# A fused attention and mixture-of-experts layer: sums of key blocks added in pairs on GpSimd, router input turned by DMA

## The reference

```python
x = x + tanh(g_xattn) * attention(layernorm(x), ctx)   # softmax(Q K^T / sqrt(32)) V, then Wo
x = x + tanh(g_ffn) * moe(layernorm(x))                # top-2 of 8 experts, capacity 1229 of 8192 places
# moe: probs = softmax(x @ Wr + br); gates, ids = top_k(probs, 2); each expert silu(x W1 + b1) W2 + b2
```

## Time and profile before

| | |
|---|---|
| median of 3 runs | 1811.75 us (1811.48 to 1812.64) |
| the profiled execution, its own time | 1810.6 us |
| its span (first to last instruction) | 1808.9 us |
| attention, start to last product of it on TensorE | 0 to 902.6 us |
| busy TensorE, VectorE, ScalarE, GpSimd | 96%, 60%, 44%, 24% of the span |
| matmul records | 10371 |

### The profile page before, as it was taken

One profiled execution on the slowest core, in us unless ns is written; L12 is line 12 of the kernel. 1 busy time (PEld: TensorE's weight loads), 2 busy tenths in 40 slices (PEclk: granted clock), 3 DMA queues, 4 the chain that ended last, 5 costly groups with the idle time before them and its releaser, 6 DMA issues.

```text
span 1808.9 us, 29536 instructions
## 1 busy us (share of the span) xinstructions
PE 1727.7 (96%) x10371; PEld 827.7 (46%) x10371; DVE 1076.8 (60%) x2087; ACT 798.2 (44%) x1093; POOL 434.4 (24%) x424
## 2 busy tenths in 40 slices
PE   6999999999999999999918999999999999999998
PEld 4324243342423334243305657475665647565563
DVE  6777867778776777867687625345252525434231
ACT  4553735547364554735423426153342516244240
POOL 2332434224343332431201211211021121112101
PEclk9999999999999999999958999999999999999999
DMA  6334263433425433243123542625263362626312
GB/s 227 106 86 125 71 167 113 102 119 100 144 93 142 137 93 116 81 114 109 42 100 105 133 124 100 168 87 154 71 174 80 120 148 88 179 50 177 75 44 29
DMA packets 214608, 203.19 MB, mean 112 GB/s; under 512 B 121813, under 2 KB 162913, under 8 KB 210457
## 3 DMA queue, kind: packets, MB, share of 16 engines
q1 hardware_dynamic: 193432, 181.80, 33.1%
q0 software_dynamic: 21120, 20.67, 6.6%
HBM read 134.57 MB, written 43.63 MB: 99 GB/s over the span
## 4 chain that ended last, share of the span: by engine, by line
PE 84%; DVE 10%; issue 3%; ACT 2%; POOL 1%; DMA 0%; SPq 0%; DVEq 0%; ACTq 0%; POOLq 0%
PE psum L1598 23%; PE psum L1574 21%; PE psum L1369 7%; PE psum L1376 6%; PE psum L1360 6%; PE psum L1350 6%; PE psum L1340 6%; PE psum L1462 5%; PE psum L1387 3%; DVE mx L938 2%; DVE reached L1092 1%; DVE x2hl L1012 1%; DVE x2hl L1014 1%; DVE stats L890 1%; DVE x2n L897 1%
## 5 line engine op out<-in xcount | busy, mean ns | idle before, releaser
L1598 PE MATMUL psum<-w,hT 128*128 128x512 f16 (+1 forms) x1920 | 415.7, 379 | 0.0
L1574 PE MATMUL psum<-xgT,w 128*128 128x308 f16 (+1 forms) x3072 | 408.1, 293 | 0.6 <-DVE xgT L1193 0.6
L938 DVE TENSOR_REDUCE mx<-psum 128x1 f32<-128x512 f32 x512 | 330.2, 683 | 104.1 <-PE psum L1350 102.5
L1574 PEld LDWEIGHTS psum<-xgT,w 128*128 128x128 f16 x3072 | 296.2, 97 | 109.3 <-DVE xgT L1193 1.1
L788 ACT ACTIVATE pt<-psum 128x1024 f32<-128x1024 f32 x256 | 255.0, 1022 | 116.4 <-PE psum L1360 116.4
L1598 PEld LDWEIGHTS psum<-w,hT 128*128 128x128 f16 (+1 forms) x1920 | 199.3, 104 | 213.8
L864 ACT ACTIVATE h<-psum,b1c 128x308 f32<-128x308 f32 (+1 forms) x256 | 117.9, 511 | 342.0 <-PE psum L1574 341.6
L1214 DVE TENSOR_TENSOR hT<-h,hT 128x615 f16<-128x615 f32 x128 | 102.5, 801 | 210.1 <-ACT hT L867 210.1
L681 POOL DMA_INDIRECT out_dram<-y,idx_now x40 | 87.6, 2191 | 498.8 <-DVE y L1246 305.8
L1243 DVE SCALAR_TENSOR_TENSOR y<-psum,b2b 128x512 f32<-128x512 f32 (+1 forms) x40 | 27.7, 691 | 269.4 <-PE psum L1598 269.4
L1340 PE MATMUL psum<-actT,wT 128*128 128x512 f16 x768 | 177.6, 379 | 2.0 <-DVE wT L925 2.0
(11 more groups left out here) (198 smaller groups left out, 1522.7 us busy)
## 6 DMA issues: line engine op xcount, KB each, us to landing
stage<-in_L_ffn_W_dram SPq DMA_DIRECT2D x62, 1024.0 KB, 5.9
stk<-qk_rows SPq DMA_DIRECT2D x192, 128.0 KB, 2.5
qk_rows<-qks SPq DMA_DIRECT2D x64, 256.0 KB, 2.5
xin<-in_x_dram SPq DMA_DIRECT2D x8, 1024.0 KB, 5.3
cin<-in_ctx_dram SPq DMA_DIRECT2D x8, 1024.0 KB, 7.5
xres<-in_x_dram SPq DMA_DIRECT2D x8, 1024.0 KB, 5.6
out_dram<-xres SPq DMA_DIRECT2D x32, 256.0 KB, 2.1
x_split<-x2hl SPq DMA_DIRECT2D x32, 256.0 KB, 2.3
```

The costliest lines, as they stand in the source:

```text
L938: v.reduce_max(mx[:, KT * t + qt:KT * t + qt + 1], ps, AX.X).then_inc(read, 1)
L1574: mm = t_.matmul(psum[:, (2 * m + ch) % 4, 0:c1 - c0], w1[:, wp, kt, m * P:(m + 1) * P], xgT[:, KT * xp + kt, c0:c1], start=(kt == 0 and ( ...
L1598: mm = t_.matmul(psum[0:rows, Y_BANK[i], :], hT[:, hp, k, c * P:c * P + rows], w2[:, wp, k, :], start=(k == 0 and (hp, wp) == (0, 0)), sto ...
```

## The change

1. The exponentials get five units of room in place of two (`pt_units`: `pt`, and the tiles `qk32`, `x2nT` and `x2n`, each once its own contents are used up).
2. For the first eight units GpSimd adds the two units of a pair (four additions of 128x512 float32 a pair, 16 a batch), and TensorE multiplies four pair sums with the ones in place of eight units. The ones products stand at slots 10, 12, 14 and 16 for the pairs and 17 to 22 for the other eight units, two of them in each of slots 18 and 20. In slots before 16 they stand between the halves of `less_maxima`, and `with_values` moves to the end of the slot.
3. Normalising the next batch's input moves from GpSimd to VectorE, slots 5 and 6; the residual's bias adds come behind the pair adds on GpSimd.
4. The reciprocals of 128x512 sums (which repeat in 32 rows) become: a transposition in 32x32 blocks on VectorE, the reciprocal of 16 numbers a row, and a transposition back with a broadcast.
5. The router: SP turns the halves `x2hl` by four DMA transposes, behind `stack_heads` of block 5 and ahead of group 0's maxima; `parts` becomes twelve float16 products, and waits for the four DMAs. The sixteen TensorE transposes and ScalarE's four copies go. The last batch's logits, behind attention, stay as they were.

```diff
+PAIRS, PT_UNITS = 4, 5
+SUMS = {10: (("pair", 0),), 12: (("pair", 1),), 14: (("pair", 2),), 16: (("pair", 3),), 17: (("unit", 8),),
+        18: (("unit", 9), ("unit", 10)), 19: (("unit", 11),), 20: (("unit", 12), ("unit", 13)),
+        21: (("unit", 14),), 22: (("unit", 15),)}
+GROUP_NORM = [16, 18, 20, 23]
+GROUP_SPLIT = [17, 19, 21, 23]
+X_NORM_SLOT = (5, 5, 6, 6)
...
# SP, batch
                 for i in range(QK_FIRST + 2):
                     stack_heads(sp, b, i)
+                if not first:
+                    sp.wait_ge(x2hl_ready, KT * b)
+                    settle(sp)
+                    for tt in range(KT):
+                        sp.dma_start(x2T[:, :, tt * P:(tt + 1) * P], x2hl[:, tt, :], transpose=True).then_inc(x2T_in, 16)
                 for g in range(NG):
...
# GpSimd, batch
+                for p in range(PAIRS):
+                    if p % 2 == 0:
+                        pool.wait_ge(mrow_ready, NG * b + (p // 2 + 2))
+                    pool.wait_ge(pv_done, UNITS * b + (2 * p + 1))
+                    for hf in range(2):
+                        copied(pool, use, ("ST", 2 * p + 1, hf), b)
+                        for j in range(2):
+                            into = pt_units[2 * p % PT_UNITS][:, hf, j, :]
+                            g.tensor_tensor(into, into, pt_units[(2 * p + 1) % PT_UNITS][:, hf, j, :],
+                                            ALU.add).then_inc(pair_added, 1)
...
# ScalarE, before the exponential of unit u
-                            act.wait_ge(pv_done, UNITS * b + max(u - 1, 0))
+                            if u < PT_UNITS:
+                                act.wait_ge(sums_done, SUM_COUNT * b)
+                                act.wait_ge(qk_split, NQ * b + NQ)
+                            else:
+                                act.wait_ge(sums_done, SUM_COUNT * b + (sum_of_unit(u - PT_UNITS) + 1))
...
# VectorE
+                    v.transpose(turned_sums[:, :], sums).then_inc(sums_turned, 1)
+                    own = mx[:, NT // 2 * g:NT // 2 * g + NT // 2]
+                    v.reciprocal(own, turned_sums[:, :].rearrange("p (c k) -> p c k", k=32)[:, :, 0:1].rearrange(
+                        "p c k -> p (c k)")).then_inc(sums_inverted, 1)
+                    v.transpose(osum[:, g % 2, 1, :].rearrange("p (c k) -> p c k", k=32),
+                                own.rearrange("p (c o) -> p c o", o=1).to_broadcast((P, NT // 2, 32))).then_inc(rinv_done, 1)
...
# TensorE, parts
+                    if first:
+                        pe.wait_ge(wr_split, 1)
+                    else:
+                        pe.wait_ge(x2T_in, 16 * KT * b)
+                    for xp, wp in PARTS:
+                        for kt in range(KT):
+                            last = t_.matmul(dst[32 * kt:32 * kt + 32, :], wr_hl[:, wp, kt, :], x2T[:, KT * xp + kt, :],
+                                             start=((xp, wp) == (0, 0)), stop=((xp, wp) == (1, 0)))
...
# TensorE, a slot
                     less_maxima(u, 0)
+                    if s < UNITS:
+                        with_ones(s)
+                        scores(s, 2)
+                    less_maxima(u, 1)
+                    scores(s, 3)
...
+                    with_values(s - LAG_C)
                     if s >= UNITS:
-                        less_maxima(u, 1)
-                        with_values(s - LAG_C)
-                    else:
-                        with_values(s - LAG_C)
-                        scores(s, 2)
-                        less_maxima(u, 1)
-                        scores(s, 3)
-                    with_ones(s - LAG_C)
+                        with_ones(s)
                     filling(s, 1)
```

More of the change, by code:

```diff
@@ L591, in batch @@
                     if i == QK_FIRST + 2:
+                        if not last:
+                            for tt in range(KT - 1):
+                                inverse_deviation(0, tt, KT * b + (KT + tt))
                         pool.wait_ge(mrow_ready, NG * b + 1)
+                    if i == QK_FIRST + 3 and not last:
+                        inverse_deviation(0, KT - 1, KT * b + (2 * KT - 1))
                     pool.wait_ge(qk32_ready, NQ * b + i + 1)
@@ L717, in _, with logit_parts, logits @@
             copied(act, pre, "bias")
[L719 to L734, removed]
+            s.activation(wr_hl[:, 0, :, :], wr[:, :, :], ACT.Copy, scale=SW).then_inc(wr_hi, 1)
+            def logit_parts(b):
+                ps, read = filled(act, use, "lg_parts", b)
+                s.activation(lg_parts[:, :], ps, ACT.Copy, scale=1.0 / SW).then_inc(read, 1)
+            def logits(b):
+                ps, read = filled(act, use, "lg", b)
+                settle(act)
+                s.activation(lg[:, b, :], ps[:, 0:KT * E], ACT.Copy).then_inc(read, 1)
             def batch(b, last):
-                rows, parts, logits = router_copy(use, b, b)
                 def queries_keys(i):
@@ L771, in batch @@
                         queries_keys(i)
[L772 to L773 removed]
                     if t == PARTS_SLOT:
[L775 removed]
+                        logit_parts(b)
                     if t < LAG_B:
@@ L992, in batch @@
                     if not last:
+                        for tt in range(KT):
+                            if t == X_NORM_SLOT[tt]:
+                                normalise(0, tt, KT * b + (KT + tt), xin[:, tt, :], xn[:, tt, :], xn_ready)
                         if LN_SLOT <= t < LN_SLOT + KT:
@@ L1295, in _, with batch @@
                 copied(pe, pre, ("w", 3, kt))
[L1297 to L1312 removed]
+            def batch(b, last_batch, first=False):
+                def parts():
+                    if first:
+                        pe.wait_ge(wr_split, 1)
+                    else:
+                        pe.wait_ge(x2T_in, 16 * KT * b)
+                    dst, full = claim(pe, use, "lg_parts", b)
+                    for xp, wp in PARTS:
+                        for kt in range(KT):
+                            last = t_.matmul(dst[32 * kt:32 * kt + 32, :], wr_hl[:, wp, kt, :], x2T[:, KT * xp + kt, :],
+                                             start=((xp, wp) == (0, 0)), stop=((xp, wp) == (1, 0)))
                     last.then_inc(full, 1)
                 def logits():
[L1317 to L1318 removed]
+                    copied(pe, use, "lg_parts", b)
+                    dst, full = claim(pe, use, "lg", b)
                     for tt in range(KT):
@@ L1322, in logits @@
                     last.then_inc(full, 1)
-                return rows, parts, logits
-            def batch(b, last_batch, first=False):
-                rows, parts, logits = router(use, b, KT * b)
                 def queries_keys(i, halves=range(2)):
@@ L1396, in filling @@
                         queries_keys(i, (half,))
-                    if s == X2T_SLOT:
-                        rows((2 * half, 2 * half + 1))
                     if (s, half) == (PARTS_SLOT, 1):
@@ L1422, in batch @@
                         copied(pe, use, ("v", 2), b)
-                        copied(pe, use, ("x2T", 3), b)
                     if 0 <= u < UNITS and u % 4 == 0:
@@ L1435, in batch @@
                                 copied(pe, use, ("v", 3), b)
-                                copied(pe, use, "lg", b)
                             else:
```

113 lines of the change are left out of this document (55 added, 58 removed).

## The result

| | before | after |
|---|---|---|
| median of 13 runs each | 1811.75 us (1810.19 to 1812.64) | 1816.41 us (1809.87 to 1819.13) |
| ratio after/before | | 1.002, 95% interval 1.0011 to 1.003 |
| profiled execution, its own time | 1810.6 us | 1810.66 us |
| its span, its mean granted clock | 1808.9 us, 0.981 | 1808.9 us, 0.976 |

The median is 0.4 us from the forecast of 1816.0, and the ratio's interval (1.0011 to 1.003) lies above 1 and around the 0.2% that a measurement can tell: the kernel after is slower by 4.7 us, which is just clear of no change. The point is right and the working behind it is not: two terms were wrong by 10 us and more, in opposite directions.

A forecast was written before the change was run, and what follows sets the result against it. The prediction took TensorE's own work to bound slots 7 to 22 and VectorE slots 2 to 4. It summed -35.2 + 12.8 - 1.6 + 28.2 = +4.2 us on 1810.6, and 1.15 for the median: 1816.0 us, range 1798 to 1829.

The forecast's parts named there:

- Slots 7 to 22: Attention slots: fewer ones products save 35.2 us in slots 7 to 15; slots 16 to 22 cost 12.8 more.
- The bound by the maxima: Slots 7 to 15: the third score waits for VectorE's maxima, so a slot without ones product takes 3.13 us, not 2.83.
- rival (d): Slots 7 to 15: scores are no bound, six slots at 2.83 us give -14, 1802 us; no separate chance given.
- `parts` -1.6: Router products on TensorE: `parts` goes from 1.00 us to 0.8 as twelve float16 products, -1.6 us over 8 batches.
- The stall, +28.2: TensorE ahead of `parts`: waits for the four router DMAs, 3.5 us in batches 2 to 6, +28.2 us in all.
- `parts` stood at 277.89: Batch 2 before the change: time of `parts` on TensorE, set against the fourth DMA's landing at 281.4, a 3.5 us wait.
- rival (a): Ahead of `parts`: router DMAs land before it, so no stall; 28.2 us less, 1788, or 1802 with half; chance 0.17.
- Slot 2 emptied: nothing: Slot 2: taking out sixteen transposes frees 1.9 us of TensorE, but VectorE has no gap, so no time is gained.
- rival (b): DMA stalls ahead of `parts` also lower TensorE's clock, some 3 us a fall, +6 to +21, 1822 to 1837; chance 0.20.

The follow-up runs named there:

- experiment 6: The changed kernel with the router of before: TensorE transposes in slot 2, products in slot 4, logits in slot 5, no transposing DMAs; 1787.76 us.
- experiment 5: The changed kernel with `parts` and `logits` put back from slots 5 and 6 to slots 4 and 5; 1819.11 us.
- experiment 2: The changed kernel with eight more products of 128x512 in slot 2 of every batch, which nobody reads; 1813.73 us.
- Experiment 1: The changed kernel with ScalarE's logits copy in slot 6 moved behind the exponentials of unit 0; 1797.86 us.

## Why the prediction came out, and where it was wrong

**Slots 7 to 22, -22.4 us forecast: right.** Without the logits' lateness (experiment 6) they gave -24.5. By its steps: a slot without a ones product 3.15 us (3.13), with one 3.93 (3.94), GpSimd's first pair 0.17 late (0.3), four adds 4.96 us (5.1), two more ones products +1.68 in slots 16 to 22 (+1.6), VectorE's block transpositions 0.70 and 0.71 us (0.7). The bound by the maxima, which rival (d) denied, is there.

**`parts` -1.6: right.** Twelve products take 285.20 - 284.43 = 0.77 us (0.8).

**The stall, +28.2: wrong place.** The step that failed is "`parts` stood at 277.89": it moved to slot 5's end, half-way to where the DMAs land. What was measured is 1.07 us in batch 2 and +11.1 for slots 2 to 6 of all batches, with falls of the clock and the saved `parts` in it, for +26.6 forecast. Landing time and issue had been read rightly (7.73 us from block 5's last issue to `parts`, 7.45 in experiment 5, for 7.5). On the rate of such DMAs the prediction had cited the Trainium skill ("DMA: Bandwidth & Descriptors", Latency and other measured facts) with an effective 261 GB/s. The trace differs: four of 256 KB take 5.46 us to issue, 192 GB/s by an estimate from that, near the 187 of the earlier trace rows. So the stall shrank as in rival (a), and not by an overlap or by quick DMAs, but by a constant.

**"Slot 2 emptied: nothing": wrong.** It is nothing in length and not for the clock (experiment 2). I had sought rival (b), stalls that cost the clock, behind the DMA wait. In the changed kernel no fall stands there, and experiment 5, with the longer stall, has four. What I hadn't thought of is a fall where TensorE keeps working thinly: 0.81 busy of 2 us. The price of (b), 3 us a fall, was too high: a fall cost 1.2 to 1.7 us. The Trainium skill ("TensorE: Matmul & The Clock Gate", A second HAM failure mode: psum-queue depth-cycling) tells of such small idling between groups of products that cycle through PSUM banks; slot 2's two banks and the falls agree with it. The section on DMA waits, which I had cited, fits the four falls of experiment 5.

**Missing term: ScalarE's logits copy, +9.6 us, and its clock falls.** The moved step was the same pair of constants. Of a moved step I had counted TensorE's and SP's queues and not ScalarE's, where a copy that waits for TensorE's last work of slot 6 stands ahead of exponentials that could run. Experiment 1 prices it at 18.6 us in the medians.

**The sum.** Forecast +4.2, profiled +0.1, medians +4.7. The stall was 15.5 too large in slots 2 to 6; the adds' stages came out 10.0 dearer (logits copy and two falls, -12.4 measured for -22.4), the start 1.3; more falls in the median run are likely the rest. Two errors met, and a forecast that hits for such reasons is worth no more than one that misses.

Open is why only some batches have a fall at the same pattern of work; the clocks and times differ from run to run, and no trace here shows by what.

## What to carry to other kernels

When a step moves, list its instructions on every engine's queue, and look for a small copy whose producer is late and behind which large work waits: a copy of 0.2 us cost 1.2 us a batch here. Before you take "idle" work off TensorE, look at what share it leaves busy there; free work may be what keeps the clock. And make the halves of a two-part change separately: here parts 1 to 4 were worth -24.4 us and part 5 took it back, and the kernel with the first half alone (1787.76 us) is 1.3% faster than the one before.

## What the runs showed of the hardware

- The granted clock fell to 1.2 GHz without a long stall: four score products, idle 0.98, 0.21, 0.21 and 0.21 us ahead of them, were enough in some batches. Waits of 2.12 to 5.00 us for the DMAs were followed by one in four of seven batches (experiment 5). A fall costs 1.2 to 1.7 us of a stage here.
- GpSimd's float32 additions of 128x512 took 1.24 us each beside maxima read from PSUM and 1.5 to 1.6 beside VectorE's passes with two inputs, and those went from 0.65 to 1.77 us: both lose. The Trainium skill ("SBUF — State Buffer", two separate sides) says that the two engines take turns at one pair of ports, whole instruction by whole instruction, when VectorE has two inputs in SBUF and GpSimd reads SBUF. The trace agrees: 1.77 us is near 0.65 + 1.24 = 1.89, one pass and one addition in turn.
- Float32 products of four column groups took 1.00 us from start to start between float16 products, and 0.86 to 0.89 where another float32 one followed; turning 128x512 float32 in 32x32 blocks took VectorE 0.70 us, as long as its other passes.
